# Cross-attention kernel: other places in the unit order for the output transposes, the output projection, a bank swap for K, and a stack of Q ahead of a shift

## What is computed

```python
Q = (query @ Wq.T + bq)      # (8, 112, 256) in 16 heads of 16
K = (key_value @ Wk.T + bk)  # (8, 375, 256)
V = (key_value @ Wv.T + bv)
scores = einsum('bhqd,bhkd->bhqk', Q, K) / sqrt(16)
attn = softmax(scores, axis=-1)
context = einsum('bhqk,bhkd->bhqd', attn, V)   # back to (8, 112, 256)
x = context @ W_o.T + b_o + query
out = (x - mean(x)) / sqrt(var(x) + 1e-5) * gamma + beta
```

## Time and profile before

| | |
|---|---|
| median of 3 runs | 141.8 us (141.06 to 141.84) |
| the profiled execution | 141.58 us, of which 139.8 us span |
| busy in the span | PE 130.3, PEld 114.1, DVE 96.5, ACT 90.0, POOL 82.0 us |
| mean granted TensorE clock | 0.996 of full speed |

### The profile page before, as it was taken

The page is one execution under the profiler, slowest core; times in us unless marked ns, Lnnn a source line. Parts: engine busy times, 40 slices in busy tenths (PEclk is TensorE's granted clock), DMA queues, the critical chain, the costliest instruction groups (busy, mean ns, idle before and its releaser), DMA issues.

```text
span 139.8 us, 3936 instructions
## 1 busy us (share of the span) xinstructions
PE 130.3 (93%) x1477; PEld 114.1 (82%) x1477; DVE 96.5 (69%) x225; ACT 90.0 (64%) x187; POOL 82.0 (59%) x105
## 2 busy tenths in 40 slices
PE   4999999999989999989999999989999999999960
PEld 3899966789779988888989898979899878878720
DVE  5997799988657854876678856765687787521442
ACT  0887545288494929686766867665957758787620
POOL 8358899995542834105289967720589007498271
PEclk9999999999999999999999999999999999999998
DMA  4997685984479822671154036532270100011102
GB/s 128 324 364 257 242 259 187 288 282 118 108 183 333 235 67 75 214 224 17 58 186 150 7 103 196 202 134 72 93 273 0 44 0 5 8 36 33 38 0 66
DMA packets 16099, 19.59 MB, mean 140 GB/s; under 512 B 2624, under 2 KB 15488, under 8 KB 16080
## 3 DMA queue, kind: packets, MB, share of 16 engines
q1 hardware_dynamic: 14960, 17.42, 38.7%
q0 software_dynamic: 640, 1.64, 4.7%
q10 hardware_dynamic: 480, 0.28, 0.7%
HBM read 6.30 MB, written 0.92 MB: 52 GB/s over the span
## 4 chain that ended last, share of the span: by engine, by line
PE 73%; DVE 10%; SPq 6%; DMA 5%; issue 2%; ACTq 1%; POOLq 0%; ACT 0%; DVEq 0%
PE m_bank L882 17%; PE pv_bank L994 13%; PE mx_bank L943 12%; PE st_bank L976 12%; DVE mx L749 6%; PE m_bank L1026 4%; PE st_bank L882 3%; DMA k_stack<-k_hl 3%; PE mx_bank L1066 3%; SPq L266 3%; PE m_bank L1005 2%; PE mx_bank L976 2%; DMA q_stack<-shift 2%; SPq L358 2%; PE m_bank L903 2%
## 5 line engine op out<-in xcount | busy, mean ns | idle before, releaser
L749 DVE TENSOR_REDUCE mx<-mx_bank 112x1 f32<-112x375 f32 x128 | 63.7, 540 | 22.1 <-PE mx_bank L943 21.8
L632 ACT ACTIVATE pw<-st_bank 125x448 f32<-125x448 f32 x86 | 45.3, 546 | 18.4 <-PE st_bank L976 18.0
L943 PE MATMUL mx_bank<-k_stack,q_stack 128*112 128x376 f32 x128 | 43.7, 354 | 1.0 <-DMA k_stack<-k_hl 0.5
L976 PE MATMUL st_bank<-q_stack,k_stack 128*125 128x224 f32 x172 | 34.8, 284 | 0.6 <-DMA q_stack<-shift 0.4
L976 PEld LDWEIGHTS st_bank<-q_stack,k_stack 128*125 128x125 f32 x172 | 28.6, 186 | 4.1 <-issue 1.5
L943 PEld LDWEIGHTS mx_bank<-k_stack,q_stack 128*112 128x112 f32 x128 | 22.1, 176 | 4.5 <-DVE mx L749 1.8
L430 POOL TENSOR_TENSOR k_hl<-k_full,k_hl 128x376 fp32r<-128x376 f32 x10 | 10.0, 1002 | 20.9 <-ACT k_hl L549 20.9
L994 PE MATMUL pv_bank<-pw,v_sb 125*17 125x112 f32 x744 | 21.5, 260 | 0.0
L994 PEld LDWEIGHTS pv_bank<-pw,v_sb 125*17 125x17 f32 x744 | 16.7, 97 | 3.1 <-issue 1.9
L882 PE MATMUL m_bank<-w_hl,c_hl 128*125 128x256 f32 x126 | 18.2, 282 | 0.0
L882 PEld LDWEIGHTS m_bank<-w_hl,c_hl 128*125 128x125 f32 x126 | 17.3, 186 | 0.0
(11 more groups left out here) (113 smaller groups left out, 177.7 us busy)
## 6 DMA issues: line engine op xcount, KB each, us to landing
k_stack<-k_hl SPq DMA_DIRECT2D x48, 188.0 KB, 2.7
c_raw<-ctxT SPq DMA_DIRECT2D x7, 375.0 KB, 4.3
q_stack<-q_hl SPq DMA_DIRECT2D x9, 112.0 KB, 2.2
x_space<-x_nat SPq DMA_DIRECT2D x4, 224.0 KB, 3.1
out<-yo SPq DMA_DIRECT2D x8, 112.0 KB, 2.0
pw<-wT SPq DMA_DIRECT2D x2, 256.0 KB, 4.3
q_stack<-q_hl POOLq DMA_DIRECT2D x3, 168.0 KB, 2.8
q_stack<-q_hl SPq DMA_DIRECT2D x3, 168.0 KB, 2.8
```

Of the source, the lines that this page charges most:

```text
L632: nc.scalar.activation(p_tile[0:KC, n % PR, :, :], st_of(n)[0:KC, 0:4 * Q].rearrange("p (j q) -> p j q", j=4), ACT.Exp, scale=float(DK) ** ...
L749: nc.vector.tensor_reduce(mx[b % 2][:, h % 2, q_pair(h // 2):q_pair(h // 2) + 1], mx_bank[n % MR][0:Q, 0:KV], axis=AX_X, op=ALU.max, negat ...
L943: nc.tensor.matmul(mx_bank[n % MR][0:Q, 0:KVP], q_stack[k][:, side, q_pair(h // 2), b - Q_STACKS[k][0], :], k_stack[b % 3][:, h // 2, :], ...
L976: last = nc.tensor.matmul(st_of(n)[0:KC, k * 2 * Q:(k + 1) * 2 * Q], k_stack[i % 3][:, 2 * g + k, c * KC:(c + 1) * KC], q_stack[qk][:, :, ...
```

## The change

OT of batch i-1 moves from unit 6 to unit 5 (unit 4 in batch 6, unit 5 in batch 7). OUT of batch i-2 follows it there at once, with its layer norm at unit 7; before, OUT of batch i-3 stood at unit 0 of the next batch. In batch 6, OUT stands at unit 8 with the layer norm at unit 8, in batch 7 the layer norm of batch 5 at unit 5. MT of batch i+1 stands at unit 7 for i = 1 to 5 (unit 4 for i = 6), and each of these transposes stands in front of the products with V of its unit. MT of batch b carries ONT of batch b-2, for b = 2 to 6, so ScalarE's `take_o_norm_t` is issued at unit 8. ONT of batches 5 and 6 stands at unit 8 of the next batch and is taken at unit 9. In the lists of the banks, the two halves of K swap: `K(i + 3, 0)` is now in `m_bank[1]` behind V or OUT, `K(i + 3, 1)` in `m_bank[0]` behind MT. SyncE issues the six DMAs of Q's last stack ahead of the shift of batch 4. GpSimd adds b_o to rows of x at the start of its share of a batch instead of at the end. No operation is added or removed.

```diff
--- before.py
+++ after.py
@@ -52,12 +52,12 @@
 PR = 3 * NC
 MR = 3
 
-U_OUT, U_OT, U_Q, U_CONTEXT = 0, 6, 11, 5
+U_OT, U_Q, U_CONTEXT, U_LN = 5, 11, 5, 7
 U_K = ((9, 11), (8, 10))
 U_V = (2, 3, 4)
 HALF = UNITS // 2
-NORM_WITH = {3: 0, 4: 1, 5: 2, 6: 3, 7: 5}
-U_MT = (8, 7, 6, 6, 6, 6, 5)
+NORM_WITH = {b: b - 2 for b in range(2, B - 1)}
+U_MT = (8, 7, 7, 7, 7, 7, 4)
 
 
 EARLY_HEADS = 16
@@ -70,19 +70,19 @@
 M0_JOBS = [("K", 0, 0), ("V", 0, 0), ("K", 1, 0), ("K", 2, 0), ("V", 2, 0), ("Q", 2, 0), ("K", 3, 0)]
 M1_JOBS = [("K", 0, 1), ("V", 0, 1), ("K", 1, 1), ("K", 2, 1), ("MT", 0, 1), ("V", 2, 1), ("Q", 2, 1), ("MT", 1), ("K", 3, 1)]
 for _i in range(1, B - V_AHEAD):
-    if _i >= 3:
-        M1_JOBS.append(("OUT", _i - 3))
     M0_JOBS.append(("V", _i + V_AHEAD, 0))
     M1_JOBS.append(("V", _i + V_AHEAD, 1))
+    M0_JOBS.append(("OT", _i - 1))
+    if _i >= 2:
+        M1_JOBS.append(("OUT", _i - 2))
     M0_JOBS.append(("MT", _i + 1))
-    M1_JOBS.append(("OT", _i - 1))
     if _i + AHEAD < B:
-        M0_JOBS.append(("K", _i + AHEAD, 0))
-        M1_JOBS.append(("K", _i + AHEAD, 1))
+        M1_JOBS.append(("K", _i + AHEAD, 0))
+        M0_JOBS.append(("K", _i + AHEAD, 1))
     if _i in (1, 2):
-        M0_JOBS.append(("Q", 3, _i - 1))
-M0_JOBS += [("OT", 5), ("MT", 7), ("OT", 6), ("OT_LAST", 0), ("OT_LAST", 2)]
-M1_JOBS += [("OUT", 3), ("ONT", 4), ("OUT", 4), ("OUT", 5), ("ONT", 6), ("OUT", 6), ("OUT", B - 1)]
+        M1_JOBS.append(("Q", 3, _i - 1))
+M0_JOBS += [("OT", 5), ("ONT", 5), ("OT", 6), ("ONT", 6), ("OT_LAST", 0), ("OT_LAST", 2)]
+M1_JOBS += [("MT", 7), ("OUT", 4), ("OUT", 5), ("OUT", 6), ("OUT", B - 1)]
 S0_JOBS += [("ONT_HALF", 0), ("ONT_HALF", 1)]
 S1_JOBS.append(("OT_LAST", 1))
 JOBS = (M0_JOBS, M1_JOBS, S0_JOBS, S1_JOBS)
@@ -364,13 +364,13 @@
                         stack_k(i + V_AHEAD, t)
                 if i + AHEAD + 2 < B:
                     load_context(i + AHEAD + 2)
+                if i == 3:
+                    for side in range(2):
+                        stack_q(sp, 3, side)
                 if i + 1 < B:
                     stack_shift(i + 1)
                 if i == 0:
                     stack_q(sp, 2, 0)
-                if i == 3:
-                    for side in range(2):
-                        stack_q(sp, 3, side)
                 if 1 <= i <= B // ROWS:
                     load_rows(i - 1)
                 if i >= 3:
@@ -476,6 +476,8 @@
                 if i == 1:
                     pool.wait_ge(st_full, UNITS + 4)
                     load_rest()
+                if 2 <= i < 2 + B // ROWS:
+                    bias_into_x(i - 2)
                 if i + AHEAD + 1 < B:
                     context_lo(i + AHEAD + 1)
                 if i == 0:
@@ -483,8 +485,6 @@
                 if i + AHEAD < B:
                     for t in range(2):
                         subtract_k(i + AHEAD, t)
-                if 2 <= i < 2 + B // ROWS:
-                    bias_into_x(i - 2)
                 if i == 2:
                     clear_q()
             for b in range(B - V_AHEAD - 3, B - 1):
@@ -655,10 +655,8 @@
                     if i + 1 < B and u == min(U_MT[i] + 1, UNITS - 1):
                         if i + 1 in NORM_WITH:
                             take_o_norm_t(NORM_WITH[i + 1], "MT", i + 1)
-                    if u == 3 and i == 6:
-                        take_o_norm_t(4, "ONT", 4)
-                    if u == 6 and i == B - 1:
-                        take_o_norm_t(B - 2, "ONT", B - 2)
+                    if u == 9 and i >= B - 2:
+                        take_o_norm_t(i - 1, "ONT", i - 1)
                     if u == 9 and i == B - 1:
                         take_first_half()
             act.wait_ge(pv_done, NG * B)
@@ -806,18 +804,12 @@
                         q_lo_part(2, u - 6)
                     if u == U_Q and i in (1, 2):
                         q_lo_part(3, i - 1)
-                    if u == U_OUT + 1 and i >= 3:
-                        layer_norm(i - 3 if i < B - 1 else B - 3)
                     if i + 1 < B and u == U_MT[i]:
                         take_shift(i + 1)
-                    if u == U_OT and 1 <= i <= 5:
+                    if u == (U_OT if i != B - 2 else 4) and i >= 1:
                         normalise(i - 1)
-                    if u == 4 and i == 6:
-                        normalise(5)
-                    if u == 5 and i == 6:
-                        layer_norm(4)
-                    if u == 4 and i == B - 1:
-                        normalise(B - 2)
+                    if u == (U_LN, 8, 5)[max(0, i - (B - 3))] and i >= 2:
+                        layer_norm(i - 2)
                     if u == 8 and i == B - 1:
                         layer_norm(B - 2)
                     if u == 8 and i == B - 2:
@@ -1093,6 +1085,14 @@
                         out_project(B - 2)
                     for h in heads[:1]:
                         scores_for_max(h)
+                    if i + 1 < B and u == U_MT[i]:
+                        transpose_max(i + 1)
+                    if u == (U_OT if i != B - 2 else 4) and i >= 1:
+                        transpose_o(i - 1)
+                    if u == (U_OT if i != B - 2 else 8) and i >= 2:
+                        out_project(i - 2)
+                    if u == 8 and i >= B - 2:
+                        transpose_o_norm(i - 1)
                     if i == B - 1 and u in (5, 8, 11):
                         values(i, u // NC - 1)
                     elif n >= SINGLE and u % NC == 1 + (n > LATE) and not (i == B - 1 and u > 2):
@@ -1103,22 +1103,6 @@
                     if i == 0:
                         for kind, *at in FIRST_JOBS.get(u, ()):
                             projects[kind](*at)
-                    if u == U_OUT and i >= 3:
-                        out_project(i - 3 if i < B - 1 else B - 3)
-                    if u == 2 and i == 6:
-                        transpose_o_norm(4)
-                    if u == 3 and i == 6:
-                        transpose_o(5)
-                    if u == 5 and i == 6:
-                        out_project(4)
-                    if i + 1 < B and u == U_MT[i]:
-                        transpose_max(i + 1)
-                    if u == U_OT and 1 <= i <= 5:
-                        transpose_o(i - 1)
-                    if u == 4 and i == B - 1:
-                        transpose_o(B - 2)
-                    if u == 6 and i == B - 1:
-                        transpose_o_norm(B - 2)
                     if u == UNITS - 1 and i == B - 1:
                         transpose_last(0)
                     if i + V_AHEAD < B and u in U_V:
```

## The result

| | median us | span of the profiled execution |
|---|---|---|
| before | 141.49 (141.06 to 141.84, 4 runs) | 139.8 us of 141.58 |
| changed | 148.82 (148.72 to 149.01, 4 runs) | 147.1 us of 148.91 |

The changed kernel takes 1.053 times as long (95% interval 1.050 to 1.056). It is slower, as forecast; but at 148.82 us, where 147.1 was forecast, it lies just above the range, which ended at 148.6.

What follows compares the result with a forecast made beforehand. TensorE's own list was taken to bound the kernel, with ScalarE's exponential bounding batch turns. Terms 3.84 + 2.4 + 0.2 + 0.25 - 0.5 - 0.66 + 0.25 = 5.8 us gave 147.4, stated as 147.1 us; range 144.2 to 148.6.

Steps and rivals of the forecast that it cites:

- 1): K's second half, batches 1 to 4: waits until ScalarE has taken ONT, a new wait of 1.06 us, four times.
- 2): Turns without OUT: 6.01 us from K's first half to unit 1's scores, exponential-bound; 3.84 us over four, K's wait included.
- 3): OUT at unit 5: no wait hides it, 0.8 us each in batches 2 to 4, 2.4 us; batch 5 loses 0.2.
- 4): MT with ONT: K's first half in batch 1 starts 0.25 us later; batch 2 loses a wait, -0.5 us.
- 5): Q's stack ahead of the shift: the wait for K's stack in batch 4 goes, -0.66 us.
- 6): Batches 5 and 6: shift 0, at most 1 us; MT at unit 4 waits 0.25 us; moves in batches 6 and 7, 0.
- B: Rival: ScalarE takes ONT before TensorE reaches K's second half, so its claim is met in time; 143.1 us, chance 0.08.
- C: Rival: claim met and the turn not bound by the exponential, so OUT costs the same anywhere; 139.7 us, chance 0.05.
- D: Rival: the shift of batch 6 lands late by 1 us; 148.1 us, chance 0.06.
- E: Rival: TensorE's clock falls in the new idle time, one 5 us stretch at 1.2 GHz; 152 us, chance 0.02.

Runs made afterwards that it cites:

- a1: Changed kernel with ScalarE's `take_o_norm_t` in front of `take_k` at unit 8 instead of behind it: 144.61 us.
- e1: Kernel before with K's halves swapped, other banks, MT of batch 3 and Q's stack moved; `take_o_norm_t` behind `take_k`: 141.17 us, against 140.27 with it in front.
- c3: Changed kernel with `take_o_norm_t` in front of `take_k` and OUT of batches 0 to 3 back at unit 0, batch 0's in `m_bank[0]`: 144.17 us.
- d1: Changed kernel with MT of unit 7 moved behind the products with V for i = 1 to 5: 151.39 us.
- b1: Kernel before with only Q's last stack issued ahead of the shift and GpSimd's b_o additions at the start of its share: 141.30 us, ratio 1.0006.
- t2: Changed kernel with ONT of batch 6 at unit 7 of batch 7 instead of 8, taken by ScalarE at unit 7 instead of 9: 148.24 us.
- a3: Changed kernel with all steps of batches 6 and 7 back where the kernel before had them: 146.65 us.

## Why the prediction was right or wrong

1) *The claim of K's second half: right.* Four waits, each a step 0.93 us too long (1.09 in batch 1), against 1.06 in the sum; undone by a1 (-4.2 us) and made alone by e1 (+0.9 us). TensorE starts 0.06 us after ScalarE's end, not 0.19, which is the small excess; most of it comes back in the six matmuls, which take 1.13 us behind the wait and not 1.03.

2) *The turn bound by the exponential: right.* From S to unit 1, 5.83 us in batch 3 (5.84 and 5.83 in batches 1 and 2) against 6.01; waits of 0.70 us by the profile and a step of 1.21 instead of 0.34 us at unit 1 of batches 4 and 5. With a1 the turn is 7.14 us long with or without OUT (c3). The pieces 1b to 5a grew by 0.58 + 0.46 + 0.99 + 0.97 = 3.00 us, where parts 2 and 4 have 3.84 less 0.41 for the wait that went in batch 1, 3.43. The 0.4 us are four times 0.18 too much from S to unit 1, less 0.1 three times, since the scores of unit 1 also take that much longer behind a wait. One row was misread here: the 0.19 us from 85.59 to 85.78 in the kernel before aren't ScalarE's handover. The head behind OUT takes a step of 0.36 us there without a wait, and where OUT is gone the scores start 0.04 us after the exponential's end. From the end of K's second half to unit 1 ScalarE bounds at 1.81 us (88.09 to 89.90), not 1.95; with OUT it was TensorE's own list that took 1.95. OUT at unit 0 was almost free, as the prediction says: 7.18 us from 3b to 4a with it, 7.14 without it (a1).

3) *OUT at unit 5: its size against the kernel before right (0.76 and 0.87 us in batches 3 and 5; 0.8), its meaning half right.* Putting OUT back doesn't return that, since it covers the normalisation (c3). I had named the cover for K's bank, and it held; d1 shows what it costs when it fails, 0.8 us a batch, where I had 0.1 to 0.3.

4) *Batch 1 and batch 2: right.* 1a to 1b grew by 0.75 us (MT's work and its wait), 2a to 2b by 0.31 us, where OUT adds 0.8 and the lost wait takes 0.5.

5) *Q's stack ahead of the shift: right in the trace, wrong as a term.* The piece 4a to 4b grew by 0.09 us only, where its neighbours grew by 0.76 and 0.87: the 0.7 us are gone against the profiled execution. But the second trace of the kernel before doesn't have that wait, and b1's median shows no gain. I took one row with a landing far above its line's median (4.8 against 2.7 us) for the landing of every execution; 0.66 us is what the order was worth in that one.

6) *Batches 5 and 6: the step that failed.* "The moves of OUT, OT and ONT in batches 6 and 7 keep PE full either way: 0", and 0.25 us for MT: together 0.25 us, measured 1.72. I counted PE's work and the banks of the scores there, and not where the steps of ScalarE stand in its own list: L622 behind an exponential that waits for PE, and OUT waiting for L622. That list alone made 0.95 us (t2), MT's place 0.28 (t1), and 0.67 us are shown by a3 as a whole but not split. The shift of batch 6 came in time, and batch 5 as a whole (0.87 - 0.55) was 0.3 us where I had 0.2.

The sum by pieces: 7.33 us, against 5.8. Of the difference, 1.47 us are part 6 and 0.38 us the start, in which the change has no part; parts 1 to 4 were 0.4 us too high, and batch 5 0.1 too low. So the range was missed by part 6; that it was missed by 0.2 us only owes something to parts 1 to 4 erring the other way. The rivals fell with the first trace: B and C need the claim to be met (C's 139.7 us also takes off 1.9 us of waits where the prediction counts 1.6 at most), D's late shift didn't come, and the granted clock of E stayed at its upper level, 2.4 GHz, in the windows with the new holes:

```profile
82.00:91.00 9.00, 7.53 (x108) 6.38 (x110) 5.99 (x15) 6.04 (x14) 5.35 (x7) 1.00 0.34 108
121.00:124.00 3.00, 2.61 (x32) 2.06 (x32) 2.12 (x6) 2.16 (x4) 0.00 (x0) 1.00 0.03 5
135.00:138.00 3.00, 2.27 (x30) 1.51 (x18) 0.00 (x0) 2.67 (x8) 2.73 (x4) 1.00 0.00 0
```

That holds for idle stretches of about 1 us, such as these. The rule in the Trainium skill ("TensorE: Matmul & The Clock Gate", Part 1) that idle time throttles the clock isn't contradicted; no hole here set it off.

## What to carry to other kernels

When two jobs share a buffer, the order in which the reading engine has the read in its own list decides, not the order of the jobs: a short read queued behind another that waits for the same producer turns a 0.6 us step into a 1 us hole, and swapping the two lines takes it away. Price a moved step in every engine's list, the last stretch of the kernel included, and look for what the step was covering where it stood. Before a wait for a DMA enters a sum, look whether its landing is near the line's median; if not, the wait may not be there in the next execution, and a second trace of the same kernel tells.

## What the runs showed of the hardware

Transfers of one kind, 188 KB each, landed 2.2 to 4.9 us after their issue within one execution. Among the six of one stack the slowest took 4.8, 3.6 and 4.3 us in three traces, beside others of 2.2 to 2.8: the slow landing came back each time, its size didn't.

The pieces of the schedule behind the start repeat within 0.06 us from trace to trace. The start doesn't, and the difference lies in TensorE's first twelve matmuls on K: 2.14 us to the next group in one trace of the kernel before and 3.12 in the other. Nothing is waited for in either, the single matmul takes 332 ns in median in one and 460 in the other, and the granted clock reads 1.00 in both; why they take longer isn't shown. From that next group to V's products of 1a it is 33.4 and 33.2 us.

Behind a wait the six matmuls of K take 1.13 us to the next row instead of 1.02, and two score matmuls 0.32 instead of 0.21.
